# Laying the query and key strips of a channel attention by transfers through DRAM, and its output products in two halves

## The reference, cut to what matters

```python
x = x + jnp.tanh(g_xattn[0]) * _L0_xattn_ref(_layernorm(x), ctx_2048, mask, mask, Wq, bq, Wk, bk, Wv, bv)

# in _L0_xattn_ref: channels (SIZE = 128, 16 heads of 8) are rows, the 256 features are positions
q = jnp.einsum('oc,bct->bot', Wq, target) + bq[None, :, None]     # k and v from the source
dot = jnp.einsum('bhdt,bhds->bhts', q, k) / math.sqrt(HEAD_DIM)
mask = target_mask[:, :, :, None] * source_mask[:, :, None, :]
dot = mask * dot - (1.0 - mask) * NEG
amap = jax.nn.softmax(dot, axis=-1) * mask
out = jnp.einsum('bhts,bhds->bhdt', amap, v)
```

## Time and profile before

| | |
|---|---|
| time, median of 3 runs | 1764.23 us (1762.54 to 1769.84) |
| the profiled execution | 1761.46 us, its span 1759.6 us |
| PE busy | 1676.9 us (95% of the span) |
| DVE, ACT, POOL busy | 1139.4, 992.1, 584.2 us |
| DMA queue of SP (q1) | 41619 packets, 71.09 MB, 12.8% of 16 engines |
| this stage | first scores from 27.4 to 271.5 us of the span |

### The profile page before, as it was taken

How to read it: one execution, slowest core, us unless ns; L and a number is a source line. 1 busy time by engine, 2 the same in 40 slices (tenths; PEclk the granted TensorE clock), 3 DMA queues, 4 the chain that set the end, 5 groups by cost and what they waited for, 6 DMA issues and landing times. The chain is left out here.

```text
span 1759.6 us, 34328 instructions
## 1 busy us (share of the span) xinstructions
PE 1676.9 (95%) x11824; PEld 1419.5 (81%) x11832; DVE 1139.4 (65%) x2540; ACT 992.1 (56%) x2502; POOL 584.2 (33%) x638
## 2 busy tenths in 40 slices
PE   7999997798999999999999999999999998899997
PEld 6666664368788988889898989888898997689985
DVE  6888888897556656656566655555555567954434
ACT  2788875686545555545556555545545543555553
POOL 4444426435511111112122111111111212877774
PEclk9999997899999999999999999999999999999999
DMA  6011122102100100100100011001000004443448
GB/s 209 14 31 32 32 81 96 60 1 101 52 13 13 45 5 14 49 1 13 37 25 25 13 65 37 13 1 37 13 1 13 1 1 122 146 120 118 127 114 291
DMA packets 50371, 95.95 MB, mean 55 GB/s; under 512 B 10838, under 2 KB 30598, under 8 KB 49216
## 3 DMA queue, kind: packets, MB, share of 16 engines
q1 hardware_dynamic: 41619, 71.09, 12.8%
q0 software_dynamic: 7584, 21.37, 4.1%
q10 hardware_dynamic: 1000, 1.26, 0.2%
HBM read 73.85 MB, written 19.25 MB: 53 GB/s over the span
## 5 line engine op out<-in xcount | busy, mean ns | idle before, releaser
L2358 POOL TENSOR_TENSOR hold_wq<-hold_wq,ca_rsum 128x512 f32<-128x512 f32 x128 | 133.9, 1046 | 797.9 <-DVE ca_rsum L2600 797.9
L2218 ACT ACTIVATE hold_wq<-ca_pT 128x512 f32<-128x512 f32 x128 | 76.4, 597 | 381.3 <-PE ca_pT L2425 381.3
L1116 DVE TENSOR_REDUCE a_mx<-a_s 128x2 f32<-128x512 f32 x256 | 164.1, 684 | 37.5 <-PE a_s L959 37.1
L2581 DVE COPY ca_values<-ca_v 128x512 f32<-128x512 f32 x128 | 88.4, 690 | 125.0 <-PE ca_v L2377 124.3
L2375 PE MATMUL ca_qk<-early_x,cw_wqkv_h 128*128 128x512 f32 x384 | 161.0, 419 | 1.3 <-PEq L1577 1.3
L2590 DVE TENSOR_TENSOR hold_wq<-ca_s,hold_wk 128x512 f32<-128x512 f32 x128 | 88.3, 690 | 108.1 <-PE ca_s L2418 105.2
L845 ACT ACTIVATE a_prob<-a_s 128x512 f32<-128x512 f32 x256 | 138.1, 594 | 34.3 <-PE a_s L979 30.8
L2377 PE MATMUL ca_qk<-early_x,cw_wqkv_l 128*128 128x512 f32 x384 | 151.7, 395 | 0.0
L2376 PE MATMUL ca_qk<-early_x,cw_wqkv_h 128*128 128x512 f32 x384 | 151.2, 394 | 0.0
L2498 PE MATMUL ca_acc<-ca_wo_h,ca_oT_l 128*128 128x256 f32 x512 | 145.2, 284 | 0.0
L2497 PE MATMUL ca_acc<-ca_wo_l,ca_oT_h 128*128 128x256 f32 x512 | 145.0, 283 | 0.0
(11 more groups left out here) (540 smaller groups left out, 4667.2 us busy)
## 6 DMA issues: line engine op xcount, KB each, us to landing
early_big<-slot_results SPq DMA_DIRECT2D x16, 512.0 KB, 7.1
mw_raw<-in_d_expert_w SPq DMA_DIRECT2D x12, 352.0 KB, 5.1
mw_down<-in_d_expert_d SPq DMA_DIRECT2D x1, 2816.0 KB
a_wraw<-a_heads SPq DMA_DIRECT2D x17, 128.0 KB, 2.0
token_rows<-early_rows SPq DMA_DIRECT2D x1, 2176.0 KB, 15.3
hold_wk<-in_c_wkT SPq DMA_DIRECT2D x1, 2064.0 KB
hold_wq<-in_c_wqT SPq DMA_DIRECT2D x1, 2064.0 KB, 8.2
a_heads<-a_osb SPq DMA_DIRECT2D x64, 32.0 KB
```

Source lines behind the costliest of these rows:

```text
L1116: dve.tensor_reduce(mx[:, b % 2, :, h], s1_bank(b, u)[:, :, :], AX.X, ALU.max)\
L2358: pool.tensor_tensor(prob[:, k % 2, :, :], prob[:, k % 2, :, :], rsum[:, k % 2, :].unsqueeze(2).broadcast_to([P, GB, TOKENS]), ALU.mult)\
```

## The change

From batch 3 on q and k are projected once, in natural row order, with weights gathered by POOL (`natural_weights`): one join (`join`, 6 products, and 2 of bias) instead of four pieces (24 and 8), one rounding (`round_pair`) and one rest (`rest_pair`). SP stores the high and low parts in a DRAM tensor `strips` in strip order (`send_parts`, six transfers of 128 KB), and loads whole strips into `qs` and `ks` (`load_strips`, two transfers of 512 KB), which takes the place of the repeated rows. Mask rows (eight transfers) and zero rows (two, and two more in iteration 1) are written to DRAM once. The output product is issued in two halves in neighbouring double slots, values are projected in slots 5 and 13, `close` and `invert` move by two slots, and POOL prepares a batch in one go at slot 0.

```diff
+        low = s.sb("low", [P, 2, 2, DIM], F32R)
+        mrow = [t[0:BATCHES, A_BUFS - 1, :, :] for t in (qs, ks)]
+        mfull = low[0:BATCHES, 0, :, :].bitcast(F32)
+        whn, wln, bextn = (s.sb(n, [P, 2, P], F32R) for n in ("whn", "wln", "bextn"))
+        strips = nc.dram_tensor("a_strips", (2, BATCHES, A_ROWS, P // A_HD * DIM), F32, kind="Internal").ap()
...
-        CLOSING, INVERTED = 35, 9
+        CLOSING, INVERTED = 37, 11
...
+        def joined(t):
+
+            b = WHOLE_ROWS if t == U * (WHOLE_ROWS - 1) else (t - JOIN) // U + 2 if (t - JOIN) % U == 0 else -1
+            return b if WHOLE_ROWS <= b < BATCHES and (b > WHOLE_ROWS or t == U * (WHOLE_ROWS - 1)) else None
...
-            w = t - A_LAG - 3
-            if w >= SLOW:
-                w = w - 1 if w >= SLOW + 1 else -1
-            return (w // U, w % U // A_SLOTS) if 0 <= w < ALL and w % A_SLOTS == A_SLOTS - 1 else None
+
+            halves = []
+            for half in range(2):
+                w = t - A_LAG - (2 + half)
+                if w >= SLOW or w - half >= SLOW:
+                    w = t - A_LAG - 4
+                    if w < SLOW:
+                        continue
+                if 0 <= w < ALL and w % A_SLOTS == A_SLOTS - 1:
+                    halves.append((w // U, w % U // A_SLOTS, half))
+            return halves
...
+        JOIN, VALUES, MASKED, ZEROED = 8, (5, 13), 4, 6
...
+                def send_masks():
+                    sp.wait_ge(mrow_ready, 8)
+                    later = slice(WHOLE_ROWS, BATCHES)
+                    for k in range(2):
+                        for i in range(4):
+                            sp.dma_start(strips[k, later, 24 + i, :].rearrange("b (h n) -> b h n", n=DIM),
+                                         mrow[k][later, i, :].bitcast(F32).unsqueeze(1)
+                                         .broadcast_to([BATCHES - WHOLE_ROWS, A_HEADS, DIM])).then_inc(mrow_sent, 16)
+
+                def send_zeros(a, b):
+                    for k in range(2):
+                        sp.dma_start(strips[k, a:b, 28:32, :].rearrange("b i (h n) -> b (i h) n", n=DIM),
+                                     mext[a:b, 0:DIM].bitcast(F32).unsqueeze(1).broadcast_to([b - a, 4 * A_HEADS, DIM]))\
+                          .then_inc(zeros_sent, 16)
+
+                def send_parts(b):
+                    p, n = b % 2, b - WHOLE_ROWS + 1
+                    sp.wait_ge(qk_hi, n)
+                    for k, c in ((0, 0), (0, 1), (1, 0), (1, 2)):
+                        sp.dma_start(strips[k, b, 8 * c:8 * c + 8, :].rearrange("d (h n) -> (d h) n", n=DIM),
+                                     hi[:, p, k, :].bitcast(F32)).then_inc(hi_sent[p], 16)
+                    sp.wait_ge(qk_lo, n)
+                    for k, c in ((0, 2), (1, 1)):
+                        sp.dma_start(strips[k, b, 8 * c:8 * c + 8, :].rearrange("d (h n) -> (d h) n", n=DIM),
+                                     low[:, p, k, :].bitcast(F32)).then_inc(lo_sent[p], 16)
+
+                def load_strips(b):
+                    p, i = b % 2, (b - WHOLE_ROWS) // 2
+                    if b == WHOLE_ROWS:
+                        sp.wait_ge(mrow_sent, 128)
+                        sp.wait_ge(zeros_sent, 32)
+                    if b == ZEROED:
+                        sp.wait_ge(zeros_sent, 64)
+                    sp.wait_ge(hi_sent[p], 64 * (i + 1))
+                    sp.wait_ge(lo_sent[p], 32 * (i + 1))
+                    after(sp, s2_psum, U * (b - A_BUFS + 1))
+                    for k, t in enumerate((qs, ks)):
+                        sp.dma_start(t[:, b % A_BUFS, :, :].rearrange("p j n -> p (j n)").bitcast(F32),
+                                     strips[k, b].rearrange("p (r j) -> r p j", r=A_SLOTS)).then_inc(strip_in[p], 16)
+
                 maxima(0)
+                send_masks()
+                send_zeros(WHOLE_ROWS, ZEROED)
                 maxima(1)
+                send_parts(WHOLE_ROWS)
+                load_strips(WHOLE_ROWS)
                 for b in range(BATCHES):
...
+                    if b == 1:
+                        send_zeros(ZEROED, BATCHES)
+                    if b + 4 < BATCHES:
+                        send_parts(b + 4)
                     if b == BATCHES - 1:
                         sp.wait_ge(out_psum, A_TILES * 14)
                         tern.send_scale(sp, 0, tern.sT, tern.sraw, tern.FIRST)
                     gather(b)
                     if b + 2 < BATCHES:
                         maxima(b + 2)
+                    if b + 4 < BATCHES:
+                        load_strips(b + 4)
...
-                    if b is not None and t % U == 2:
+                    if b is not None and t % U == 0:
                         normal_x(b)
                         centre_x(b)
+                        rest_x(b)
                         centre_c(b)
-                    if b is not None and t % U == 8:
-                        rest_x(b)
                         rest_c(b)
+                    if t == MASKED:
+                        mask_rows()
+                        natural_weights()
...
+                def round_pair(b):
+                    p, i = b % 2, (b - WHOLE_ROWS) // 2
+                    act.wait_ge(qk_psum, b - WHOLE_ROWS + 1)
+                    if b < WHOLE_ROWS + 2:
+                        act.wait_ge(k_stack, 2 * WHOLE_ROWS)
+                    else:
+                        act.wait_ge(hi_sent[p], 64 * i)
+                        act.wait_ge(qk_lo, b - WHOLE_ROWS - 1)
+                    act.activation(hi[:, p, :, :], proj[0][:, :, :], ACT.Copy).then_inc(qk_hi, 1)
...
+                def join_bias(b):
+                    freed(pe, b, "q", 0)
+                    if b == WHOLE_ROWS:
+                        pe.wait_ge(natural_ready, 6)
+                    for k in range(2):
+                        pe.matmul(proj[0][:, k, :], bextn[EXT, k, :], mext[EXT, DIM * b:DIM * b + DIM],
+                                  start=(k == 0), stop=False, skip_group_check=True)
+
+                def join(b):
+                    pe.wait_ge(xl_ready, b + 1)
+                    pe.wait_ge(cl_ready, b + 1)
+                    for k, (h, l) in enumerate(((xh, xl), (ch, cl))):
+                        o = proj[0][:, k, :]
+                        pe.matmul(o, whn[:, k, :], h[:, b % 2, :], start=False, stop=False, skip_group_check=True)
+                        pe.matmul(o, whn[:, k, :], l[:, b % 2, :], start=False, stop=False, skip_group_check=True)
+                        mm = pe.matmul(o, wln[:, k, :], h[:, b % 2, :], start=False, stop=True, skip_group_check=True)
+                    mm.then_inc(qk_psum, 1)
...
+                        if u == 0 and b >= WHOLE_ROWS:
+                            pe.wait_ge(strip_in[b % 2], 32 * ((b - WHOLE_ROWS) // 2 + 1))
...
-                def weigh(b, j):
-                    pe.wait_ge(prob_ready, U * b + A_SLOTS * (j + 1))
+                def weigh(b, j, t):
...
+                def rest_pair(b):
+                    p, i = b % 2, (b - WHOLE_ROWS) // 2
+                    dve.wait_ge(qk_hi, b - WHOLE_ROWS + 1)
+                    if i == 0:
+                        dve.wait_ge(mrow_ready, 8)
+                    after(dve, lo_sent[p], 32 * i)
+                    dve.tensor_tensor(low[:, p, :, :], proj[0][:, :, :], hi[:, p, :, :].bitcast(F32), ALU.subtract)\
+                       .then_inc(qk_lo, 1)
```

More of the change, by code:

```diff
@@ L555, in bank_of @@
         def bank_of(b, kind, part):
-            return (5 * b + ORDER.index(f"{kind}{part}")) % 2
+            return (5 * b + ORDER.index(f"{kind}{part}")) % 2 if b < WHOLE_ROWS else 1
         def freed(eng, b, kind, part):
@@ new lines, in weigh @@
+                    if t == 0:
+                        pe.wait_ge(prob_ready, U * b + A_SLOTS * (j + 1))
+                        if j == 0:
+                            pe.wait_ge(v_ready, b + 1)
+                        if b == 0 and j == 0:
+                            pe.wait_ge(work.gram_lo, work.grams_to(0))
+                        if j % 2 == 0 and o is proj[0]:
+                            pe.wait_ge(work.gram_lo, work.grams_to(2))
+                        if j % 2 == 0 and o is not out:
+                            pe.wait_ge(qk_lo, BATCHES - WHOLE_ROWS)
+                            pe.wait_ge(v_ready, BATCHES)
+                        if j % 2 == 0 and o is out:
+                            after(pe, out_copied, 2 * b + j // 2 if b < BATCHES - 1 else 2 * b - 1)
@@ new lines, in weigh @@
+                    for v in range(A_SLOTS):
+                        r = (v + 2) % A_SLOTS
+                        mm = pe.matmul(o[A_ROWS * r:A_ROWS * r + A_ROWS, j % 2, :],
+                                       vT[:, b % A_BUFS, t, A_TILES * r + j, :],
+                                       prob[:, (U * b + A_SLOTS * j + v) % PR, t, :], start=(t == 0), stop=(t == 1),
+                                       skip_group_check=True)
+                    if t == 1:
```

(10 more changed lines are left out.)

137 lines of the change are left out of this document (79 added, 58 removed).

## The result

The changed kernel takes 1898.33 us (median of 4 runs, 1896.21 to 1903.42) against 1764.01 for the one before: 1.0759 times as long, 95% interval 1.0725 to 1.0793. The sign was forecast, the size was not: 134 us slower instead of 62, above the range's end of 1868.

A forecast was written before the change was run, and what follows sets the result against it. No single engine bounds the kernel before: projection, stacking and exponentials take turns; after the change SP's queue does. 47 us steady plus 7 and 8 at the start make 62 us, on the median 1826; range 1770 to 1868.

The forecast's parts named there:

- the other side of the argument: Strip loads run wide on 16 engines: 2.5 us, SP's cycle 11.9, engines set the pace, 1756 us; chance 0.12.
- SP's cycle: SP's queue per batch: 19.3 us with narrow loads against 15.05 before, 4.3 more over 11 intervals, 47 us.
- The engines' own period: Batch period if engines alone set it: 13.97 us against 15.05, a gain of 14.0 us over 13 batches.
- narrow, and worse: Rival: each engine gets less than 26.6 GB/s from DRAM and masks take the upper bound: 1860 us; chance 0.12.
- The once-only terms: Stores made once: 7 us for late second maxima and strips(3) behind mask and zero stores, 8 for later zeros.
- my 5 to 13: Zeros for batches 6 to 15, ahead of parts(5): 128 packets on ten engines, 5 to 13 us, taken as 8.
- one term of 7 us: Start: second maxima and strips(3) come late behind mask and zero stores, 3 to 17 us, taken as 7.
- No time of its own: Clock rival: TensorE may get 1.2 GHz, 0.44 us per pair becoming 0.9, inside the wait for SP; no chance given.
- the first rival: Loads run wide on 16 engines, engines set the pace: gain 14.0 less 2 to 9 at the start, 1756; chance 0.12.
- the second rival: The two loads take different engines, or 8 each: 4.9 us, cycle 14.3, gain eaten by the start, 1766; chance 0.06.
- the eleven intervals: Steady loss: 4.3 us per batch counted over the 11 intervals between the 12 iterations that load strips, 47 us.

The follow-up runs named there:

- the 3976 us: Profiled execution of the wide-load kernel without zero stores, with loads issued right behind sums and heads and `hold_wq` one iteration later: 3976 us; median of its runs 1791.31.

## Why the prediction was right in direction and wrong in size

The sign alone doesn't bear out the mechanism: with wide loads, the other side of the argument, the kernel was still 58 us slower. Three steps failed: the price of SP's cycle, the price of the stores made once, and the clock taken as costing nothing. Counted over the same slots, nine cycles of 4.3 us and two more with the 15 us of the start were forecast, 39 and 23 us, and 73 and 57 were found; behind them come 13 us for which no term stood.

**Right.** The number of engines from the outermost size (4 more packets for each load, a share of 0.24). That the loads hold the inverses and those the whole queue. The cycle as bound of the steady part, without an engine in it. The engines' own period, 13.97 forecast and 14.0 to 14.9 found at full clock. Halves of about 0.55, 0.57 found.

**SP's cycle, 19.3 forecast, 22.6 found.** Six part stores took 3.1 us, not 2.1: they cost 0.5 each, like maxima, and not 0.35, like num. From the issue of the loads to the spread 13.6, not 11.6: 22 to 23 GB/s for an engine, not the 26.6 that 16 engines reach from full rows. That was the rival "narrow, and worse" (23 GB/s), whose 1860 was still too little. The average batch was 23.2, so each cycle cost 8.1 us more than before, not 4.3.

**The once-only terms failed, 7 + 8 forecast.** The four batches from slot 16 on are 4.3, 22.3, 3.9 and 26.5 us longer than before, 57 in all, of which the steady cycle's loss explains some 8 in the fourth. The step is the price of a packet from few partitions, bounded by 0.04 and 0.1 us from a full load and from four stores of 8 partitions each in flight together. In iteration 1 it was an estimated 0.14, so 128 of them are about 18 us, not 5 to 13; SP's cycle there, from spread to spread, took 43.8 us and not 22.6, 21 more where 8 was forecast. The run with larger packets shows that it isn't their number that sets it. The Trainium skill ("SBUF — State Buffer", section on the DMA port swizzle) says that a transfer's rate depends on how many of 16 ports its partitions reach, and has 104 GB/s for partitions 0 to 15; the trace agrees in kind, with 76 GB/s while the masks are stored from 13 partitions (49 to 66 us) and 80 with the zeros. By that figure the 1.31 MB of zeros in iteration 1 would be an estimated 12.6 us, the upper end of my 5 to 13; the 18 us from the trace are more, from 10 partitions. The masks, with up to 256 packets on an engine, failed in a second way: one term of 7 us stood for the late maxima and the late strips, but TensorE waited for both, one after the other, 11.6 and 7.6 us. Behind the zeros it was the sums, for which VectorE and then TensorE stood still (17.7).

**"No time of its own" failed.** I had weighed the clock only against the wait for SP, in which 0.44 or 0.9 us for the scores is the same. But every pair of slots behind the wait needs TensorE too, and at 1.2 GHz it needs 19 us a batch. In the changed kernel's steady part that is hidden by 22.6 us of SP; at its start it is likely most of what the four waits leave of the 57 us, 16 us, which is a difference and not a measurement. In the kernels with wide loads it was the larger part of what a wait cost where the clock fell (5 us for 1.7). With the price of the zeros it also makes the first rival's time wrong: wide loads give 1822, and 1786 without the zeros, not 1756. Loads on different engines, the second rival, were not run.

**The end of the stage, 13 us, was missing.** The twelfth iteration that loads strips has a cycle too, and only the eleven intervals between the twelve were counted: its batch took 26.5 us instead of 16.3, some 7 us of it the cycle that the nine before had. `hold_wq`, 2 MB, stands in the same queue in front of it (370.60 us), and from the heads to num SP waits 4.9 us there instead of 2.0. I had listed the queue of a batch, not what is queued once. The last 3 us are in slots 240 to 254, where the clock is 0.50 up to 402.9.

Open: the masks' price by itself; whether it is the number of partitions that makes a store slow; why equal waits sometimes bring the clock down and sometimes not; the 3976 us.

## What to carry to other kernels

When work is moved from engines to a transfer queue, list all that stands behind it, also what is queued once, count every cycle that has the transfer in it, and look for the rate of a transfer from as few partitions before pricing one by its packets. A freed engine gives slack that must not turn into waits: 1.4 to 2 us of idle TensorE cost 4 to 5 us here where its clock fell, so a relief of 1 us a batch was lost by one wait in four batches. So waits of 1 to 2 us are worth taking away too, and after each move one looks which transfer now comes last.

## What was not expected of the hardware

- Stores from 13 partitions or fewer ran at 76 to 89 GB/s in all, with packets of 1 KB and of 4 KB alike; stores of 1 KB packets from 128 partitions at 283.
- Behind 1280 packets of zero rows SP's issue itself took long: 17.53 us for four stores that else take 2.03.
- A single wait of 1.35 us in the kernel before was followed by a granted clock of 0.50 for 6.8 us once, and another of 1.34 left it at 1.00. The Trainium skill ("TensorE: Matmul & The Clock Gate", section on oscillation) describes a kernel that waits for a transfer in every step and starts each at the lower clock; the traces agree, and show it for single waits.
